# A two-layer graph network on sparse neighbours: keeping x1 on the chip, writing each output row once, and another tile order in layer 2

## The reference, cut to what matters

```
h  = relu(layernorm(x))
seq = (h @ W_seq).reshape(N, 16, 32)
scores = leaky_relu(seq@a1 [:, :, None] + seq@a2 [:, None, :]) + (1 - adj) * -65500
x  = x + elu((softmax(scores) @ seq) @ W_out + b_out)          # layer 0, 16 heads
h  = relu(layernorm(x))
z  = scale * (h @ W_q.T + b_q) @ (h @ W_k.T + b_k).T * adj
z  = where(z == 0, -10000, z)
x  = x + relu(softmax(z) @ (h @ W_v.T + b_v))                  # layer 1
```

## Time and profile before

| | us |
|---|---|
| median of three runs | 493.81 |
| the profiled execution | 495.05 |
| its span | 493.1 |
| TensorE busy | 393.8 (80%) |
| VectorE busy | 368.7 (75%) |
| GpSimd busy | 260.5 (53%) |
| ScalarE busy | 244.2 (50%) |
| mean granted TensorE clock | 0.921 |

### The profile page before, as it was taken

How to read it: one execution, slowest core, us unless ns; L and a number is a source line. 1 busy time by engine, 2 the same in 40 slices (tenths; PEclk the granted TensorE clock), 3 DMA queues, 4 the chain that set the end, 5 groups by cost and what they waited for, 6 DMA issues and landing times.

```text
span 493.1 us, 6193 instructions
## 1 busy us (share of the span) xinstructions
PE 393.8 (80%) x2044; PEld 283.2 (57%) x2044; DVE 368.7 (75%) x728; ACT 244.2 (50%) x511; POOL 260.5 (53%) x267
## 2 busy tenths in 40 slices
PE   3599999994699998988499888879974738995960
PEld 3578888783488787873366555537562315542420
DVE  2998899983899998974999996997434539988300
ACT  1369877753899997923234333534423132242310
POOL 2343152246886886648466648554257766761330
PEclk9689999999699998999799999989995959898995
DMA  7968999510001333326334427512236766654450
GB/s 270 406 208 288 416 329 340 203 68 5 5 7 22 90 95 89 93 78 211 113 109 141 145 76 206 186 68 86 86 122 197 185 157 149 130 112 57 57 70 4
DMA packets 27259, 70.03 MB, mean 142 GB/s; under 512 B 8153, under 2 KB 8409, under 8 KB 25049
## 3 DMA queue, kind: packets, MB, share of 16 engines
q0 software_dynamic: 13056, 38.45, 29.6%
q1 hardware_dynamic: 13904, 31.16, 17.7%
q10 hardware_dynamic: 264, 0.00, 0.0%
HBM read 52.47 MB, written 17.13 MB: 141 GB/s over the span
## 4 chain that ended last, share of the span: by engine, by line
POOL 21%; DVE 18%; issue 18%; PE 12%; DMA 2%; ACT 1%; DVEq 0%; POOLq 0%; ACTq 0%
POOL s_shared L1210 7%; PE psum L1372 6%; PE psum L1277 4%; POOL out_dram L1221 4%; DVE s_shared L786 3%; DVE s_shared L779 3%; DVE s_shared L777 3%; POOL s_rs L1220 3%; POOL s_shared L1230 2%; DVE w_seq L968 2%; DVE s_x L793 2%; POOL s_x L1226 2%; POOL s_shared L1191 2%; DVE h_t L1012 1%; DMA w_out<-h_dram,s_near_rank 1%
## 5 line engine op out<-in xcount | busy, mean ns | idle before, releaser
L1047 ACT ACTIVATE s_shared<-psum,seq_all 128x320 bf16<-128x320 f32 x192 | 81.7, 567 | 13.4 <-PE psum L1257 7.3
L1277 PE MATMUL psum<-s_shared 128*128 128x198 bf16 x768 | 76.5, 257 | 11.4 <-POOL s_shared L1191 11.4
L1277 PEld LDWEIGHTS psum<-s_shared 128*128 128x128 bf16 x768 | 69.0, 99 | 19.6 <-POOL s_shared L1191 10.4
L547 PE MATMUL psum<-w_seq,hT 128*128 128x272 f32 x256 | 63.0, 401 | 0.4 <-ACT w_seq L414 0.4
L1299 PE MATMUL psum<-w_out,hT 128*128 128x512 f32 x128 | 58.8, 603 | 0.0
L1321 PE MATMUL psum<-w_qk,s_early 128*128 128x257 f32 x240 | 55.7, 385 | 0.0
L547 PEld LDWEIGHTS psum<-w_seq,hT 128*128 128x128 f32 x256 | 48.8, 195 | 10.1 <-ACT w_seq L414 0.5
L1321 PEld LDWEIGHTS psum<-w_qk,s_early 128*128 128x128 f32 x240 | 45.3, 194 | 6.4
L1210 POOL DMA_INDIRECT s_shared<-seq_dram,tab x30 | 36.9, 1232 | 13.7 <-issue 8.9
L266 POOL TENSOR_TENSOR rstd<-veps,power 128x1 f32<-128x1 f32 x16 | 8.9, 559 | 60.8 <-DVE veps L458 60.8
L1191 POOL TENSOR_TENSOR s_shared<-s_shared 128x1056 f32<-128x1056 f32 x16 | 31.1, 1945 | 16.3 <-DVE s_shared L779 16.2
(11 more groups left out here) (253 smaller groups left out, 758.1 us busy)
## 6 DMA issues: line engine op xcount, KB each, us to landing
adj_ring<-in_adj_dram SPq DMA_DIRECT2D x16, 1024.0 KB, 7.6
seq_dram<-seq_all POOLq DMA_DIRECT2D x16, 264.0 KB, 4.2
x_ring<-in_x_dram SPq DMA_DIRECT2D x16, 256.0 KB, 8.2
h_dram<-h_t SPq DMA_DIRECT2D x16, 256.0 KB
w_seq<-in_L_gnn_W_seq_dram SPq DMA_DIRECT2D x1, 1024.0 KB, 7.2
w_q<-in_L_gnn_W_q_dram SPq DMA_DIRECT2D x1, 1024.0 KB, 13.8
w_k<-in_L_gnn_W_k_dram SPq DMA_DIRECT2D x1, 1024.0 KB, 16.0
w_v<-in_L_gnn_W_v_dram SPq DMA_DIRECT2D x1, 1024.0 KB, 9.6
```

What stands on the lines that cost most here:

```text
L547: last = pe.matmul(bank[2 + 2 * (t % 2) + i][:, 0:SX // 2], hT[:, t % 2, c * P:(c + 1) * P], w_seq[:, c, i * (SX // 2):(i + 1) * (SX // 2) ...
L1047: last = act.activation(ind[i][:, j, PAD:], bank[4 + i][:, 0:LN], ACT.Sign, bias=seq_all[:, j, D + n:D + n + 1])
L1277: last = pe.matmul(acc(i)[:, k, 0:3 * W2], ind[i][:, j, k * P:(k + 1) * P], rhs.rearrange("p t w -> p (t w)"), start=(j == 0 and k != 1), ...
```

## The change

1. Start. a1 and a2 are loaded as two rows of 128 bytes, spread over the partitions by a TensorE product with ones, and picked by VectorE (three small operations). Before its first real work TensorE runs 8 matmuls of 512 columns on a zeroed tile, and 8 more behind the spreading product; GpSimd zeroes that tile first. Eight more such matmuls follow the two broadcasts at the start of block 2.
2. The five scatters leave the end of block 1; the first 8 rounds of block 2 issue two each. The table wait and the early loads move from round 6 to round 9, with 4 x tiles in place of 8; four x tiles are loaded in the first-layer loop (`X_LATE`).
3. First-layer loop: the 16 scatters of x1 to `out` go; 9 gathers stand before the loop in place of 8, the others move by a tile or so.
4. Layer 2: tile order SEQ1 = 0 1 2 3 4 6 8 10 12 14 11 13 15 9 7 5, four score groups, all 40 gathers in one run, then 16 puts as plain scatters of the finished x1 tile. ScalarE's Relu is gone; VectorE's `add_x` takes Relu(bank) + x1, and a product may reuse a bank after `add_x` of four places before. The queries of tiles 12 to 15 all stand before the products.

```diff
+                pool.memset(warm[:, :], 0.0).then_inc(warm_set, 1)
...
-                for t in range(SCATTERED):
-                    pool.indirect_dma_start(record_dram[:, :], ...rank[:, t:t + 1]...).then_inc(rec_stored, 16)
...
-                    act.dma_start(a_col[:, k:k + 1],
-                                  a_d.rearrange("(d o) -> d o", o=1).partition_broadcast(P // DH)).then_inc(a_loaded, 16)
+                    act.dma_start(a_row[:, k, :], a_d.rearrange("(o d) -> o d", o=1)).then_inc(a_loaded, 16)
...
-                act.wait_ge(a_loaded, 2 * 16)
+                act.wait_ge(a_set, 1)
...
                 ln(0)
                 ln_bias(0)
+                dve.wait_ge(a_spread, 1)
+                step(dve.tensor_tensor(a_own[:, :, :], bank[7][:, 0:2 * DH]..., own_dim[:, :]..., ALU.mult))
+                dve.tensor_reduce(a_col[:, :], a_own[:, :, :], AX_X, ALU.add).then_inc(a_set, 1)
                 ln(1)
...
+                for _ in range(WARM):
+                    pe.matmul(bank[6], warm[:, 0:P], warm[:, :])
+                pe.wait_ge(const_ready, 1)
+                pe.wait_ge(a_loaded, 2 * 16)
+                pe.matmul(bank[7][:, 0:2 * DH], ones[0:1, :], a_row...).then_inc(a_spread, 1)
+                for _ in range(WARM_2):
+                    pe.matmul(bank[6], warm[:, 0:P], warm[:, :])
...
-                    if n < 5:
-                        scatter(SCATTER[n], SCATTER[n + 1])
-                    if n == 6:
+                    if n < T // 2:
+                        scatter(2 * n, 2 * n + 2)
+                    if n == AHEAD_FROM:
...
                     pool.tensor_tensor(rs[:, t % 2, :], ve[:, t % 2, :], power[:, :], ALU.pow).then_inc(rstd_ready, 1)
-                    pool.indirect_dma_start(out[:, :], ...own[:, SEQ[t], :]..., x1[:, t, :], None).then_inc(x1_stored, 16)
...
+                def add_x(p):
+                    own_x = x1[:, TURN[SEQ1[p]], :]
+                    dve.wait_ge(o_done, p + 1)
+                    dve.scalar_tensor_tensor(own_x, bank[2 + p % 4], 0.0, own_x, ALU.max, ALU.add).then_inc(o_added, 1)
...  (VectorE's list in layer 2)
+                constants(0, EARLY); dots 0 1 2 3; scores1(0); h_sum copy; normalise1(0); aggregate1 0 1 2 3
+                dots 6 8 10 12; constants(EARLY, T); dot(14); scores1(1); dots 11 13; normalise1(1)
+                aggregate1 6 8; dot(15); scores1(2); aggregate1(10); normalise1(2)
+                add_x 0 1; aggregate1(12); add_x(2); dot(9); aggregate1(14); add_x(3); dot(7); aggregate1(11); add_x(4)
+                dot(5); scores1(3); aggregate1(13); add_x(5); normalise1(3); aggregate1(15); add_x(6)
+                aggregate1(9); add_x(7); aggregate1(7); add_x(8); aggregate1(5); add_x 9 to 15
...  (GpSimd)
-                for t in range(9):
-                    gather1(t)
-                for t in range(T):
-                    put(t)
-                    if 9 + t < T:
-                        gather1(9 + t)
+                for t in SEQ1:
+                    gather1(t)
+                for p in range(T):
+                    t = SEQ1[p]
+                    pool.wait_ge(o_added, p + 1)
+                    pool.indirect_dma_start(out[:, :], ...own[:, t, :]..., x1[:, TURN[t], :], None).then_inc(out_stored, 16)
...  (TensorE)
-                        pe.wait_ge(o_ready, t - 3)
+                        pe.wait_ge(o_added, t - 3)
```

More of the change, by code:

```diff
@@ L1026, in _ @@
                     aggregate1(t)
-                for g in range(1, len(PARTS)):
-                    t0, n = PARTS[g]
-                    if g > 1:
-                        for t in range(PARTS[g - 1][0], t0 - 1):
-                            aggregate1(t)
-                    scores1(g)
-                    if g > 1:
-                        aggregate1(t0 - 1)
-                    normalise1(g)
-                for t in range(*(PARTS[-1][0], T)):
-                    aggregate1(t)
+                for t in (6, 8, 10, 12):
+                    dot(t)
+                constants(EARLY, T)
+                dot(14)
+                scores1(1)
+                dot(11)
+                dot(13)
+                normalise1(1)
+                aggregate1(6)
+                aggregate1(8)
+                dot(15)
+                scores1(2)
+                aggregate1(10)
+                normalise1(2)
+                add_x(0)
+                add_x(1)
+                aggregate1(12)
+                add_x(2)
+                dot(9)
+                aggregate1(14)
+                add_x(3)
+                dot(7)
+                aggregate1(11)
+                add_x(4)
+                dot(5)
+                scores1(3)
+                aggregate1(13)
+                add_x(5)
+                normalise1(3)
+                aggregate1(15)
+                add_x(6)
+                aggregate1(9)
+                add_x(7)
+                aggregate1(7)
+                add_x(8)
+                aggregate1(5)
+                for p in range(9, T):
+                    add_x(p)
             @block.scalar
@@ L1261, in _ @@
                 broadcast(1)
+                for _ in range(WARM_3):
+                    pe.matmul(bank[2], ones_b[:, :], bias_rows[:, 0, 0:D])
                 pe.wait_ge(pad_set, 2)
@@ L1346, in _ @@
                 pe.matmul(bank[0], ones[:, 0:P], h_acc).then_inc(h_sum_mm, 1)
-                queries(13)
+                for t in range(EARLY, T):
+                    queries(t)
                 def transposes1(k):
-                    if SLOTS[k]:
+                    if SLOTS[SEQ1[k]]:
                         pe.wait_ge(agg_ready, with_slots[k + 1])
```

206 lines of the change are left out of this document (112 added, 94 removed).

## The result

The changed kernel takes 507.84 us (median of 4, 505.0 to 515.11) against 493.88 (median of 4): 1.029 times the time before, 95% interval 1.023 to 1.034. It is 14 us slower by the medians; 483.5 was forecast. The profiled execution took 505.0, its span 503.2, so the two traces differ by 10 us.

The account below looks back on a forecast made before the run. Block 1 and the first-layer loop were read as bound by VectorE's search and work, layer 2 by its waits. 495.05 - 3.6 - 3.4 - 1.3 - 0 - 2.0 = 484.75, as a median 483.5 us; range 476.5 to 495.

Parts of the forecast that it names:

- Part 1, the start: Start of block 1: products start some 6 us earlier and VectorE's x waits go, -3.6 us (bounds -3.6 to -1.2).
- Part 2, the scatters: End of block 1: without GpSimd's five scatters it ends 3.4 us earlier, their cost covered in block 2's rounds; -3.4 us.
- Rival D: Start and rounds: the start does not move the search, or scatters in the rounds are not covered; 490 us, chance 0.05.
- Parts 3 and 4: Warm-up matmuls shorten block 2's first rounds, -1.3 us; the first-layer loop, VectorE's, keeps its length, 0 (-5 to +1.3).
- Part 5, layer 2: Layer 2, engines placed by earlier durations without the old hole: ends 2 us earlier, -2.0 (bounds -12 to +13).
- the hole of before: Layer 2 of the kernel before: ScalarE, TensorE and VectorE waited 9.89, 9.94 and 12.56 us, cause not shown by the trace.
- rival A: Layer 2: the hole comes again, 13 us on one engine; 487.5 to 496.5, middle 492 us, chance 0.17.
- the placing: Layer 2's engines laid out by earlier durations, first gather at 362.99: last gather lands near 418.7, last put corrected to 475.
- Rival B: Layer 2: products waiting for `add_x` of four places before decide, slower than before; 501.5 us, chance 0.09.
- Rival E: Layer 2: each gather is held for a VectorE dot (0.69 us), 19 more gathers, 13 us; 496 us, chance 0.03.

Follow-up runs that it names:

- experiment 3: The kernel before with all 40 gathers of layer 2 ahead of the first put, otherwise unchanged: 511.06 us, ratio 1.037.
- experiments 1: The changed kernel with GpSimd waiting for landing after six of layer 2's gathers, so no run is longer than 8: 489.03 us, ratio 0.990.
- 9: The changed kernel with a GpSimd memset of 576 columns behind every 5th gather of layer 2, no wait for landing: 483.42 us, ratio 0.981.
- experiment 10: The changed kernel with a memset of 64 columns behind each of layer 2's 40 gathers: 504.26 us, ratio 1.022.
- experiment 7: The changed kernel with the first 20 gathers of layer 2 fetching 128 columns of 512, a quarter of the bytes: 515.96 us, ratio 1.049.
- 12: The changed kernel with a 576-column memset behind each 5th layer 2 gather and VectorE's first four adds moved up: 477.9, 493.3, 501.5, 501.9 us.

## Why the prediction was wrong

- *Part 1, the start:* right in mechanism. x waits fell from 3.6 to 0.2 as put; what was missed is that the first x tile and the first search also start 1.5 us earlier (10.15 in place of 11.67). VectorE reaches its `count_b` at 102.49 in place of 107.59: -5.1 where -3.6 was put.
- *Part 2, the scatters:* right, mis-sized. The 3.4 us between GpSimd and ScalarE was taken alone; the start of the next block behind it was held at 2.9 us, and is 0.89 when the last work is not a scatter. -10.56 + 5.1 = -5.5 in place of -3.4. Rival D fell.
- *Parts 3 and 4:* -0.9 for -1.3, -0.7 for 0. The waits for rstd fell from 10.0 to 5.7 us, and the loop kept its length all the same, as put.
- *Part 5, layer 2:* this step failed. It was put at -2.0 and came out at +22.8. The prediction saw the hole of before, could not say what held the signals, and then wrote "I place the changed kernel without it"; it even counted the going of the puts from between the gathers as a reason against rival A. It is the reason for it. In the old order the first 21 gathers stood 1.33 us apart; from there puts stood among them, and its last late signal was taken at 404.18, in the gathers' first long pause (3.07 us, to 405.06). The change issues 40 in one run, and signals were up to 23.1 us late. Lengthening the run alone costs 17 us (experiment 3); breaking or thinning it in the changed kernel takes 19 to 24 us off (experiments 1, 9), to 0.990 and 0.981 of the time before. Rival A had the right place and too small a price, 496.5 at most: it took the hole at its old size, where its size follows the run.
- *In the placing:* the last gather's landing was put at 418.7, where 362.99 + 39 x 1.27 + 3.6 gives 416.1, and "2 us early" on 473.7 gives 475.7, not 475. Both slips are small beside the 22.8.
- *Rival B,* the bank chain, is real and small. Without late signals layer 2 took 115 to 124 us where 111 were placed; product 4 waited 14.9 to 18.2 us in the changed order where 11.5 was put; moved adds give 3.4 back.
- *Rival E,* the dots hold the gathers, came in small. In the changed kernel three gathers that were issued inside one of the first four dots took 1.19, 1.10 and 1.42 us in place of 0.95, some 0.9 us in all; the four issued beside the eight dots from 366.75 to 371.7 took 0.94 to 0.96. By the Trainium skill, "SBUF — State Buffer", section "Who interferes with whom", a VectorE instruction with two SBUF inputs contends with a GpSimd instruction that reads SBUF. This trace agrees for the first three gathers and not for the four beside the eight dots.

What stays open: through what the signals are held. Shown is that a long run of indirect DMAs does it, at 1.29 us apart in the mean (the changed kernel) and at 1.38 (experiment 10), and that it needs neither the bytes nor busy DMA engines (experiment 7), nor the change's other edits (3). It hits TensorE's signals to ScalarE, in one trace those to VectorE too (12), and by 1.2 to 1.6 us VectorE's to itself (between 380 and 387 in the changed kernel). At a mean distance of 1.56 us it is over, and 1.42 to 1.48 lies on the edge; below that, the lateness does not fall in step with the distance. Every break and every filler thins GpSimd's issuing and the packets of its gathers alike, so no run tells which of the two it is. The profile's ends of matmuls are modelled; but in the kernel before TensorE had gone on to product 2 and the transposes up to 392.0 while the signal of product 1, ended at 387.5, was taken at 394.89, so TensorE itself had moved on. The path no run shows.

## What to carry to other kernels

A hole in which several engines wait at once on signals whose senders are long done is a finding, not noise: ask what else runs through it before changing the order around it. Gathers issued in one unbroken run were cheaper on paper and dearer on the chip; a filler of 0.6 us behind every second was enough, behind every fifth it was on the edge, and in the old order it beat waiting for data to land (0.962 of the time before against 0.986). Pair each wait with its sender by the order of the lists, not by the nearest row ahead: the nearest matmuls made the waits here look shorter than they were. Price an edit by parts and run the parts: the first two of the four parts of this change were worth 12 us.

## What the runs showed that was not expected

- A signal 42 us late (queries ended at 365.0, copied at 406.90, in experiment 7); from 378 to 404 TensorE and ScalarE did nothing, and GpSimd issued gathers.
- A barrier behind GpSimd's indirect scatters opens 2.94 us after their end, one behind ScalarE's work 0.89.
- The kernel before took 493.1 to 494.5 us (medians) on four occasions and 486.5 on a fifth, there in 19 executions within 5 us. Why is open.
